# Squared-relu experts on one core: half of each down product in three passes of high and low parts

## The reference, cut to what matters

```python
x_lat = x @ fc1_w.T
h = relu2(jnp.einsum('tl,eil->eti', x_lat, w1))      # up, every expert, every token
h = h * cw.T[:, :, None]                             # weight of the expert for the token
y_lat = jnp.einsum('eti,eli->tl', h, w2)             # down, summed over the experts
routed = y_lat @ fc2_w.T
shared = relu2(x @ shared_up_w.T) @ shared_down_w.T
```

## Time and profile before

| | |
|---|---|
| three runs | 1145.95, 1141.73, 1144.16 us (median 1144.16) |
| span of the profiled execution | 1142.5 us |
| TensorE busy | 1058.0 us (93%) |
| VectorE busy | 758.7 us (66%) |
| ScalarE busy | 599.1 us (52%) |
| GpSimd busy | 561.4 us (49%) |
| 32 multiplies of `act` by the token weights, GpSimd | 75.7 us, 2369 ns each |
| 34 squares, VectorE | 41.6 us, 1222 ns each |
| 128 fp32 records of the down products, TensorE | 59.9 us |

### The profile page before, as it was taken

How to read it: one execution, slowest core, us unless ns; L and a number is a source line. 1 busy time by engine, 2 the same in 40 slices (tenths; PEclk the granted TensorE clock), 3 DMA queues, 4 the chain that set the end, 5 groups by cost and what they waited for, 6 DMA issues and landing times. The chain is left out here.

```text
span 1142.5 us, 18205 instructions
## 1 busy us (share of the span) xinstructions
PE 1058.0 (93%) x6276; PEld 891.7 (78%) x6276; DVE 758.7 (66%) x1312; ACT 599.1 (52%) x1027; POOL 561.4 (49%) x408
## 2 busy tenths in 40 slices
PE   5899999999999999999998899997977988999992
PEld 4788888888888888888886776654765787999992
DVE  4877764787556775667775644466788655777777
ACT  3566653666536665446662423433532255777772
POOL 1664622756236563355540347762314776544453
PEclk9999999999999999999999999998998989999996
DMA  7700240002400762000000146641200457666666
GB/s 196 52 28 1 58 36 3 19 11 38 56 2 24 207 218 69 1 1 1 1 2 24 58 137 212 215 136 56 106 2 6 161 191 240 207 221 219 225 212 199
DMA packets 45642, 109.94 MB, mean 96 GB/s; under 512 B 8519, under 2 KB 26069, under 8 KB 43504
## 3 DMA queue, kind: packets, MB, share of 16 engines
q1 hardware_dynamic: 38640, 95.46, 30.2%
q0 software_dynamic: 6912, 13.30, 3.1%
HBM read 94.27 MB, written 41.29 MB: 119 GB/s over the span
## 5 line engine op out<-in xcount | busy, mean ns | idle before, releaser
L422 POOL TENSOR_TENSOR at_prob<-at_prob,at_inv_sum 128x1024 f32<-128x1024 f32 x128 | 243.6, 1905 | 287.9 <-DVE at_inv_sum L647 287.9
L612 ACT ACTIVATE at_pt_h<-ps 128x512 fp32r<-128x512 f32 x256 | 139.1, 596 | 148.7 <-PE ps L537 148.6
L697 DVE TENSOR_TENSOR at_pt_l<-ps,at_pt_h 128x512 fp32r<-128x512 f32 x256 | 164.6, 685 | 60.8 <-ACT at_pt_h L612 60.7
L686 DVE TENSOR_REDUCE at_neg_max<-ps 128x1 f32<-128x1024 f32 x128 | 156.1, 1220 | 42.1 <-PE ps L41 41.7
L579 ACT ACTIVATE at_prob<-ps,at_neg_max 128x1024 f32<-128x1024 f32 x128 | 143.7, 1123 | 18.1 <-DVE at_neg_max L686 18.1
L537 PE MATMUL ps<-ident,at_prob 128*128 128x128 f32 x1024 | 133.8, 274 | 3.8 <-POOL at_prob L422 3.8
L2072 POOL DMA_INDIRECT lines<-f_y,f_x_raw x96 | 95.8, 998 | 82.7 <-ACT f_y L1990 54.7
L537 PEld LDWEIGHTS ps<-ident,at_prob 128*128 128x128 f32 x1024 | 120.0, 141 | 20.9 <-POOL at_prob L422 4.7
L39 PE MATMUL ps<-at_k_h,at_q_h 128*128 128x512 f32 x256 | 108.8, 425 | 0.0
L41 PE MATMUL ps<-at_k_h,at_q_l 128*128 128x512 f32 x256 | 100.7, 393 | 0.0
L39 PE MATMUL ps<-at_pt_h,at_v_h 128*128 128x512 f32 x256 | 100.5, 393 | 0.0
(11 more groups left out here) (308 smaller groups left out, 2541.7 us busy)
## 6 DMA issues: line engine op xcount, KB each, us to landing
e_raw<-in_we SPq DMA_DIRECT2D x32, 624.0 KB, 4.2
f_cw_row<-cw SPq DMA_DIRECT2D x32, 512.0 KB, 4.7
slots<-in_empty SPq DMA_DIRECT2D x4, 3456.0 KB, 46.3
f_x_raw<-slots SPq DMA_DIRECT2D x32, 432.0 KB, 4.8
lines<-in_empty SPq DMA_DIRECT2D x3, 2048.0 KB, 33.8
f_e_raw<-in_we SPq DMA_DIRECT2D x32, 128.0 KB, 2.8
at_wq_raw<-in_wq SPq DMA_DIRECT2D x4, 512.0 KB, 3.5
at_wo_raw<-in_wo SPq DMA_DIRECT2D x4, 512.0 KB, 3.3
```

The lines of the kernel that those rows point to most:

```text
L422: nc.gpsimd.tensor_tensor(prob[:, t % RING, :], prob[:, t % RING, :], inv_sum[:, t:t + 1].broadcast_to([P, T]), ALU.mult).then_inc(normed, 1)
L612: nc.scalar.activation(pt_h[:, e[1] % PT, :], turned(e[1]), ACT.Copy).then_inc(pt_high, 1)
L686: nc.vector.tensor_reduce(neg_max[:, t:t + 1], slot(n, start), AX.XY, ALU.max, negate=True).then_inc(maxed, 1)
L697: nc.vector.tensor_tensor(pt_l[:, e[1] % PT, :], turned(e[1]), pt_h[:, e[1] % PT, :].bitcast(F32), ALU.subtract).then_inc(pt_split, 1)
```

## The change

Of each down product, the first 512 tokens (bank 4) are made in three fp32r passes, the other 512 (bank 5) stay one plain fp32 matmul. For this

- ScalarE's step makes the high part of both weight matrices of expert n + 2 (256 columns in place of 128), and, behind it, the high part `d_h` of the first 512 columns of the weighed `act` of expert n - 2 (`HIGH_LAG` is 2);
- VectorE's step makes the low part of both weight matrices (256 columns), and, behind it, the low part `d_l` of expert n - 2, of 512 columns, from two SBUF tiles;
- TensorE waits for `act_split` (the low part `d_l`) before the down product, where it waited for `weighed`;
- the loops of ScalarE and VectorE run two steps longer;
- the token weights' transposed tile `cw_t` gets no memory of its own and lies in the last row of `cw_row`.

```diff
@@ TensorE, step
                     if known(it, r, DOWN_LAG):
                         m = (r - DOWN_LAG) % BODY
-                        pe.wait_ge(weighed, n - DOWN_LAG + 1)
+                        pe.wait_ge(act_split, down_low(n - DOWN_LAG))
 ...
-                        for b in range(NB):
-                            cols = slice(b * BANK, (b + 1) * BANK)
-                            last = nc.tensor.matmul(ps[:, 4 + b, :], e_raw[:, m, 1, :], act_of(m)[:, cols], start=first, stop=final)
-                        last.then_inc(down_done, 1)
+                        product(nc, ps[:, 4, :], e_h[:, m, 1, :], e_l[:, m, 1, :], d_h[:, m % 2, :], d_l[:, m % 2, :], first, final)
+                        nc.tensor.matmul(ps[:, 5, :], e_raw[:, m, 1, :], act_of(m)[:, BANK:], start=first, stop=final)\
+                            .then_inc(down_done, 1)
@@ ScalarE, high_weights
-                    nc.scalar.activation(e_h[:, r % BODY, :], e_raw[:, r % RAW, 0, :], ACT.Copy).then_inc(e_high, 1)
+                    nc.scalar.activation(e_h[:, r % BODY, :, :], e_raw[:, r % RAW, :, :], ACT.Copy).then_inc(e_high, 1)
@@ ScalarE, step
                     if known(it, r, 0, EXP0 - AHEAD):
                         high_weights(it, r + AHEAD)
+                    if known(it, r, HIGH_LAG):
+                        act_e.wait_ge(weighed, n - HIGH_LAG + 1)
+                        if known(it, r, HIGH_LAG + 2):
+                            act_e.wait_ge(down_done, n - HIGH_LAG - 1)
+                        m = (r - HIGH_LAG) % BODY
+                        nc.scalar.activation(d_h[:, m % 2, :], act_of(m)[:, 0:BANK], ACT.Copy).then_inc(act_high, 1)
@@ VectorE, low_weights
-                    nc.vector.tensor_tensor(e_l[:, r % BODY, :], e_raw[:, r % RAW, 0, :], e_h[:, r % BODY, :].bitcast(F32),
+                    nc.vector.tensor_tensor(e_l[:, r % BODY, :, :], e_raw[:, r % RAW, :, :], e_h[:, r % BODY, :, :].bitcast(F32),
                                             ALU.subtract).then_inc(e_split, 1)
@@ VectorE, step
                     if known(it, r, 0, EXP0 - AHEAD):
                         low_weights(it, r + AHEAD)
+                    if known(it, r, HIGH_LAG):
+                        m = (r - HIGH_LAG) % BODY
+                        dve.wait_ge(act_high, down_high(n - HIGH_LAG))
+                        nc.vector.tensor_tensor(d_l[:, m % 2, :], act_of(m)[:, 0:BANK], d_h[:, m % 2, :].bitcast(F32),
+                                                ALU.subtract).then_inc(act_split, 1)
```

More of the change, by code:

```diff
@@ L753, in squared_relu_experts_phase @@
     BODY, RAW, RING, ROWS = 8, 8, 8, 4
-    DOWN_LAG, AHEAD, REFILL = 3, 2, 4
+    DOWN_LAG, HIGH_LAG, AHEAD, REFILL = 3, 2, 2, 4
     EARLY = SH0 // 2
@@ L766, in squared_relu_experts_phase @@
         e_raw = sb("e_raw", [P, RAW, 2, P])
-        e_h, e_l = sb("e_h", [P, BODY, P], F32R), sb("e_l", [P, BODY, P], F32R)
+        e_h, e_l = sb("e_h", [P, BODY, 2, P], F32R), sb("e_l", [P, BODY, 2, P], F32R)
+        d_h, d_l = sb("d_h", [P, 2, BANK], F32R), sb("d_l", [P, 2, BANK], F32R)
         lat_h, lat_l = sb("lat_h", [P, T], F32R), sb("lat_l", [P, T], F32R)
@@ L776, in squared_relu_experts_phase @@
         cw, total = sb("cw", [P, TT, EXP0]), sb("total", [P, TT])
-        cw_t = sb("cw_t", [EXP0, T])
+        cw_t = cw_row[0:EXP0, ROWS - 1, :]
         cw_dram = net.cw_dram[0]
@@ L801, in act_of, with down_high, down_low @@
             return act[:, (r + SH0) % RING, :]
+        def down_high(n):
+            return n + (SH0 + 1)
+        def down_low(n):
+            return n + (SH0 - EARLY + 1)
         def blocks(ap):
@@ L911, in step @@
                             cols = slice(b * BANK, (b + 1) * BANK)
-                            last = product(nc, slot(1 + SH0 + r)[:, b, :], e_h[:, r, :], e_l[:, r, :],
+                            last = product(nc, slot(1 + SH0 + r)[:, b, :], e_h[:, r, 0, :], e_l[:, r, 0, :],
                                            lat_h[:, cols], lat_l[:, cols], True, True)
@@ L993, in step @@
                         nc.scalar.activation(hi[:, :, LINEAR_PIECES[k]], raw[:, :, LINEAR_PIECES[k]], ACT.Copy).then_inc(net.linear_high, 1)
-                steps(act_e, EXP0 // BODY - 1, EXP0, step)
+                steps(act_e, EXP0 // BODY - 1, EXP0 + HIGH_LAG, step)
                 act_e.wait_ge(down_done, EXP0)
@@ L1122, in step @@
                                                 ALU.subtract).then_inc(net.linear_split, 1)
-                steps(dve, EXP0 // BODY - 1, EXP0, step)
+                steps(dve, EXP0 // BODY - 1, EXP0 + HIGH_LAG, step)
                 for b in range(NB):
```

## The result

| | before | after |
|---|---|---|
| median of four runs | 1144.28 us | 1200.47 us (1200.55, 1200.38, 1182.68, 1201.95) |
| ratio | | 1.042, 95% interval 1.035 to 1.049 |
| a second set of four | 1143.24 us | 1200.78 us (1198.31 to 1201.38), ratio 1.050, 1.048 to 1.052 |
| profiled span | 1142.5 us | 1198.6 us |

The change makes the kernel slower by 56 us. Slower was forecast, but by 37: the time lies 8 us above the range. The first interval is wide because two of the four runs near 1200 were set aside as disturbed, which the second set, where all four stand at 1198 to 1201, shows they weren't. Of the eight executions seven were near 1200 and one was at 1182.68, which is nearly the forecast. That already suggests that something tips one way or the other.

What follows compares the result with a forecast made beforehand. TensorE was taken to bound the kernel at 3.107 us a step; afterwards VectorE and GpSimd take turns at 4.30. Loop +34.9, end +1.5 and start +0.3 gave +36.7 us, 1180.9 us; range from 1170 to 1192.

Steps and rivals of the forecast that it cites:

- the port: Expert loop: d_l stands until GpSimd's running multiply is over, so VectorE and GpSimd take turns; step 4.30 us.
- overlap: Expert loop on VectorE: the next square starts 0.07 us before the end of d_l's record.
- Its letter: Expert loop: if the multiply waits for the low part's very end, step 4.41 us, the whole some 3 us more.
- ScalarE had room: Expert loop: ScalarE's weight high parts, d_h and relu take 2.1 us in a step and fit.
- The pieces for the next phase: VectorE's two low parts of the next phase's weights, behind d_l, cost their own 1.15 and 0.63 us, 1.8 together.
- start of the loop: Start: the second low part at 650.47 and the square behind it come 0.3 us later.
- last square to the copy of the sums: End of the loop: 6.01 us becomes 7.5, so +1.5 us.
- the additions to x: VectorE in steps 2 and 4: two additions of 1.22 us each, now with somebody waiting, cost 2.3 us.
- the 0.3 of step 4: Expert loop, step 4: 0.3 us added because TensorE is the later one there.
- TensorE's path: Expert loop, d_l through down, up, relu to square: 4.29 us against VectorE's 4.23, so TensorE's lost gain costs or gives nothing.
- Rival 3: Expert loop: TensorE's clock falls for good through idling, step 5.8 us, +43, 1224 us; chance 0.06.
- rival 1: Expert loop: no turn-taking, TensorE stays the bound, step 2.94 us, 1140 us; chance 0.04.

Runs made afterwards that it cites:

- lag4_alone: The changed kernel with DOWN_LAG 4 in place of 3 and four buffers for the parts, d_l still from SBUF: 1180.42 us, ratio 1.032.
- experiment 1: The changed kernel with one idle fp32 matmul on TensorE between up and down product from step 7 on: 1184.82 us, ratio 1.037.
- Experiment 5: The changed kernel with DOWN_LAG 4 in place of 3: alone 1180.42 us; with d_l also made from a PSUM copy from step 8 on, 1150.9 us.
- experiment 2: The changed kernel with d_l read from PSUM bank 6 from step 5 on, output wrong: 1153.59 us, ratio 1.009.
- Experiment 8: The changed kernel with three passes for experts 4 to 29 only, d_l from PSUM copies, DOWN_LAG 4, REFILL 5, next phase's pieces behind the last step: 1140.1 us.
- copy_to_psum: The changed kernel with ScalarE copying the weighed half to PSUM from step 8 on and d_l made from that copy: 1162.9 us, ratio 1.019.

## Why the prediction was right and where it was wrong

**Right: what bounds the kernel before, and the port.** By its own terms, with the starts of the quick step (the square at 716.55 to the one at 720.79): square to low part 1.14 (forecast 1.14), to the multiply 0.16 (0.17), multiply 2.46 (2.37 and 0.13), its end to `d_l`'s end 0.56 (0.56), overlap 0.08 (0.07). The sum is 4.24 for a forecast of 4.30, and lag4_alone shows 4.25 in its steps. That its 1180.42 us is so near to 1180.9 is in part luck: from the square of expert 2 to that of expert 31 it took 124.8 us for 129.1, but the start was 1.5 and the end 1.6 longer than forecast. The Trainium skill, "SBUF — State Buffer", section "SBUF: two separate sides", says that the shared pair of ports is held for a whole instruction by whoever starts first. Beside a special mode of VectorE, it names operations with two SBUF inputs, against a GpSimd operation that reads SBUF. The traces agree on both points: `d_l` 2.84 behind a multiply of 2.47, 1.78 behind one of 1.40, 0.68 with one input in PSUM. Its letter would have made the step 4.41; by the record the multiply starts while the low part is still running, and 4.24 was measured.

**The smaller terms.** ScalarE had room, as forecast. The pieces for the next phase were sized rightly (1.21 and 0.71 us on record, forecast 1.15 and 0.63), but the 1.8 us that they were to cost didn't come. Each stands ahead of a square that is late anyway: VectorE's wait before it is 0.59 and 1.09 us in place of 1.7, and the two pairs of steps with a piece take 10.26 and 10.27 us (788.25, 798.51, 808.78), like the others. In lag4_alone, where VectorE has no such wait, they do cost: steps of 5.38 and 4.89.

**Wrong: the clock.** The table sets the sum against the trace, square to square:

| stretch | forecast | measured | difference |
|---|---|---|---|
| start of the loop, to the square of expert 2 | +0.3 | -0.27 | -0.6 |
| experts 2 to 7 | 24.1 | 25.9 | +1.8 |
| experts 7 to 31, 24 steps | 105.0 | 123.0 | +18.0 |
| last square to the copy of the sums | 7.5 | 8.06 | +0.6 |

24.1 is five steps of 4.30 with the additions to x and the 0.3 of step 4, 105.0 is 24 steps with 1.8 for the pieces. Of the 19.8 us too few, nearly all lie in the steps 7 to 31, twelve pairs of 10.25. Twelve pairs at the 8.7 to 8.8 us that experiment 1 shows at full clock, with the 1.3 us that the pieces cost there, would be 106 to 107. So 16 to 17 us of the 123.0 are the clock, and the rest of the difference is the loop through TensorE, which is longer than the 4.30 forecast. Experiment 1 takes 16 us away without touching the port or the lag. Experiment 5 ends lower still, but there the long gaps and the loop go away together, so it doesn't single out the clock.

The step that failed is the last sentence on TensorE's path: 4.29 against 4.23, "nearly equal, so the gain on TensorE is lost and costs or gives nothing". Two paths of nearly equal length are not harmless, and with a first pass of 0.34 the one through TensorE was the longer. Rival 3 (0.06) looked at the clock, with three faults. It took the idle time as 1.35 us in each step. TensorE is idle for about 2.7 us in two steps in either case (10.22 less 4.59 and 2.94; or 8.58 less twice 2.94), but once a down product is late, the next one finds its `d_l` ready and follows at once, so all the idle time comes in one piece. And it took comfort from a stretch of the earlier trace rows in which the engine is busy for 7.17 of 10 us in many small pieces. The rows right behind that stretch, in the kernel before, say otherwise:

```profile
851.53 1.94 PE L1364 MATMUL ps<-la_sc,la_v 128*32 128x128 f32 x32 [1.45 <-DVE la_sc L1554]
...
851.53:854.53 3.00, 3.00 (x48) 2.34 (x48) 0.42 (x1) 0.54 (x2) 0.00 (x0) 0.50 0.00 0
```

There the clock falls behind a gap of only 1.45 us. And the rival asked only for a clock that falls for good (5.8 a step, 1224), not for one that falls and recovers in every pair: the runs show 5.11 a step and 1200. The price of a fall, 1.65 us of TensorE's time, could have been read from the earlier trace rows: there 3.40 us at 0.51 do the work of 1.7.

The condition that the prediction gave for itself, "the clock in that stretch is below 0.95 (rival 3)", was met: 0.84.

**Wrong: the price of rival 1.** "The step is 2.94, 1140 us" was tried in experiment 2 and gave 1153.6. The same loop that had been worked out for the forecast (down, up, relu, square, `d_l`) was not applied to the rival. It is 6.59 us for two steps with the quick `d_l`. Experiment 8, which gets to 1140, takes the port, the lag and the edges of the loop together.

**Why the tipping.** In four traced executions practically the same gap in step 6 (2.17 twice, 2.16, 2.13 us) had three outcomes. Where the clock survived it, in copy_to_psum, the next gap was short (1.04 us); if it falls, the late relu makes the next gap 2.5 us, and the fall repeats. The one execution at 1182.68, with a mean clock of 0.976 over the span where the others have 0.957 to 0.963, fits that, but it was not traced. What decides it in one execution is open.

## What to carry to other kernels

Before a subtraction or copy with both inputs in SBUF is put on VectorE, look at what GpSimd runs at that time: it costs the rest of GpSimd's instruction on top of its own length (here 2.84 us in place of 0.69). A PSUM operand takes the wait away (0.68), and a GpSimd instruction cut in two shortens it (1.78). When a consumer's wait moves to a later producer, add up the whole loop through all queues and divide by the steps it spans, for every rival too: here 6.6 us over two steps hid a gain of 0.165 a step, and one more step of lag set it free. Where TensorE becomes the engine that waits, write down each single gap, price a fall of the clock behind it, and ask what a late product does to the next gap, before saying that its idle time is free.

## What the runs showed of the hardware

- The clock fell to half behind single gaps of 2.17 and 2.5 to 2.6 us in a loop where TensorE is busy three quarters of the time, and came back before the next square. With gaps of 1.05 us every 4.25 us, it stayed at 1.00. The length of a gap alone doesn't say what follows: behind 2.13 us (copy_to_psum) it stayed up, behind 1.45 us at 851.53 in the kernel before it fell. The stretch of 3 us behind one of the long gaps:

```profile
720.92:723.92 3.00, 3.00 (x6) 1.83 (x6) 3.00 (x3) 0.00 (x0) 1.84 (x1) 0.50 0.02 7
```

- A slow product can cause the next gap. Here the fall then came back in every pair of steps for 24 steps, until the loop ended. The Trainium skill, "TensorE: Matmul & The Clock Gate", section "HAM oscillation — how this bites in real kernels", describes a loop whose every tile starts at the lower clock because of the wait before it. This trace shows the same pattern, with a wait for another engine in place of a DMA, and with every second step slow instead of each one.
- Useless work on an engine that waits made the kernel 16 us faster (1200.5 to 1184.8).
